# Last feed-forward of a four-layer block: gate and up from moments of the token rows, down weights in the order of the groups

## The reference, cut to what matters

```python
def spline_reconstruct(control_points, out_size, in_size):
    idx, f = _catmull_rom_grid(control_points.shape[0], out_size * in_size)
    ...  # w: cubic in f from four neighbouring control points
    return w.reshape(out_size, in_size)
gate = jnp.einsum('bsh,ih->bsi', hidden_states, gate_w)
up = jnp.einsum('bsh,ih->bsi', hidden_states, up_w)
inter = jax.nn.silu(gate) * up
return jnp.einsum('bsi,hi->bsh', inter, down_w)
```

## Time and profile before

| | |
|---|---|
| three runs | 2403.79, 2404.9, 2405.71 us |
| profiled execution, its span | 2401.79 us, 2400.0 us |
| mean granted TensorE clock | 0.981 of 2.4 GHz |
| TensorE, its weight loads | 2245.5 us (94%), 1246.9 us (52%) |
| VectorE, ScalarE, POOL | 1133.1 (47%), 866.2 (36%), 175.4 us (7%) |
| chain that ended last | PE 81%, DVE 11%, ACT 4%, issue 2%, DMA 1% |
| last feed-forward | 2085 to 2400 us |

### The profile page before, as it was taken

The page is one execution under the profiler, slowest core; times in us unless marked ns, Lnnn a source line. Parts: engine busy times, 40 slices in busy tenths (PEclk is TensorE's granted clock), DMA queues, the critical chain, the costliest instruction groups (busy, mean ns, idle before and its releaser), DMA issues.

```text
span 2400.0 us, 25795 instructions
## 1 busy us (share of the span) xinstructions
PE 2245.5 (94%) x9444; PEld 1246.9 (52%) x9444; DVE 1133.1 (47%) x2367; ACT 866.2 (36%) x1697; POOL 175.4 (7%) x356
## 2 busy tenths in 40 slices
PE   8999999999998989999999999968877888799999
PEld 3555554556664445555555556634434555444444
DVE  1433434474223855556555557755445666411111
ACT  1323332312221644545454445533333555311111
POOL 0000100000000211111101001000000000000000
PEclk9999999998999999999999999989988999999999
DMA  5444443334523311100000122010020111000000
GB/s 221 169 142 183 174 170 139 155 126 138 185 79 110 130 42 58 59 24 23 20 26 20 32 78 96 14 35 19 10 85 13 52 52 59 12 1 9 5 9 9
DMA packets 52513, 178.88 MB, mean 75 GB/s; under 512 B 5457, under 2 KB 25233, under 8 KB 46590
## 3 DMA queue, kind: packets, MB, share of 16 engines
q1 hardware_dynamic: 50662, 139.49, 16.9%
q0 software_dynamic: 1728, 37.75, 4.1%
HBM read 121.58 MB, written 46.47 MB: 70 GB/s over the span
## 4 chain that ended last, share of the span: by engine, by line
PE 81%; DVE 11%; ACT 4%; issue 2%; DMA 1%; SPq 0%; POOL 0%; DVEq 0%; ACTq 0%; POOLq 0%
PE psum L119 64%; PE psum L112 7%; PE psum L1468 5%; PE psum L1513 4%; DVE small L2300 2%; ACT WK L2258 1%; PE psum L1056 1%; DVE R L1223 1%; PE psum L2227 1%; DVE R L1222 1%; DVE R L1794 1%; DMA R<-in_wkv 1%; DVE WK L251 0%; DVE small L228 0%; DVE WK L1213 0%
## 5 line engine op out<-in xcount | busy, mean ns | idle before, releaser
L119 PE MATMUL psum<-R,WK 128*125 128x512 f32 (+7 forms) x3536 | 1325.2, 523 | 28.4 <-DMA WK<-in_ctxT 7.4
L119 PEld LDWEIGHTS psum<-R,WK 128*112 128x112 f32 (+4 forms) x3536 | 594.6, 174 | 687.3 <-issue 566.8
L112 PE MATMUL psum<-small,WK 112*125 112x112 f32 (+5 forms) x2036 | 280.7, 267 | 90.3 <-ACT WK L2264 28.5
L112 PEld LDWEIGHTS psum<-small,WK 112*125 112x125 f32 (+5 forms) x2036 | 228.7, 154 | 192.9 <-issue 92.5
L119 PE MATMUL psum<-WK,R 128*112 128x375 f32 (+3 forms) x704 | 221.0, 453 | 10.5 <-DVE R L1794 7.0
L1644 DVE TENSOR_REDUCE small<-psum 112x1 f32<-112x487 f32 x128 | 85.0, 664 | 194.4 <-PE psum L119 191.2
L119 PE MATMUL psum<-R 128*128 128x112 f32 (+3 forms) x960 | 158.7, 309 | 17.4 <-DVE R L1794 16.2
L119 PEld LDWEIGHTS psum<-WK,R 128*112 128x112 f32 (+2 forms) x704 | 111.8, 171 | 84.7 <-issue 14.8
L119 PEld LDWEIGHTS psum<-R 128*128 128x128 f32 (+3 forms) x960 | 116.1, 184 | 56.2 <-issue 26.2
L1468 PE MATMUL psum<-R,WK 128*112 128x512 f32 x256 | 120.1, 592 | 0.0
L1563 ACT ACTIVATE WK<-psum,small 112x487 f32<-112x487 f32 x128 | 97.0, 758 | 54.1 <-DVE small L1646 53.1
(11 more groups left out here) (214 smaller groups left out, 2126.7 us busy)
## 6 DMA issues: line engine op xcount, KB each, us to landing
R<-in_wf POOLq DMA_DIRECT2D x6, 4096.0 KB, 14.1
d_w<-R POOLq DMA_DIRECT2D x6, 2048.0 KB, 18.6
R<-d_w SPq DMA_DIRECT2D x6, 2048.0 KB, 11.2
WK<-in_ctxT SPq DMA_DIRECT2D x16, 750.0 KB, 5.6
d_v<-WK SPq DMA_DIRECT2D x16, 750.0 KB
R<-in_wq SPq DMA_DIRECT2D x7, 1024.0 KB, 7.3
R<-in_wo SPq DMA_DIRECT2D x6, 1024.0 KB, 17.1
d_k<-X SPq DMA_DIRECT2D x8, 750.0 KB, 3.2
```

The lines of the kernel that those rows point to most:

```text
L112: ins = pe.transpose(dst, src, idn[0:k, 0:k])
L119: ins = pe.matmul(dst, lhs, rhs, start=k == 0, stop=k == len(pairs) - 1)
```

## The change

The 2048 rows of gate and up are sorted by where their knots lie and cut greedily into groups of at most 128 rows, whose knots in each of the four 128-column pieces fall on at most seven positions (`spline_windows`). For a group, 32 functions of the column per piece (1, q, q squared, q cubed, and the same four cut off at each of seven positions) span all rows. In the last stage TensorE first multiplies the transposed token block by these functions (`feature`: four products of 32 output partitions per group, one per piece), which gives 128 moments per token (`fT`); gate and up of the group are then one product over these 128 moments with the group's coefficient rows (`gate_up`). The dense gate and up weights are no longer built; their 80 units are gone, and 48 are left, five per iteration of stage 4. The coefficient rows are stored once (`d_feat`), fetched in the order of the groups (`load_rows`, in stage 3, ahead of `back`), spread over the positions by VectorE (`which`, `row_of`, in iterations 3 to 7 of stage 4, behind the residual add; `moments`, the functions themselves, in iteration 8), and transposed in stage 5 (`turn_rows`, `keep_columns`). POOL writes the positions (`places`). As h now comes in the order of the groups, the down weights, built as before, are stored to DRAM behind stage 4 (`store_down`) and fetched in that order in stage 6, a seventh behind the V load of each sequence from the second on (`turn_down`). In the last stage the down products are cut in four parts with the moments of the next block between them, SiLU is one ScalarE activation straight from PSUM, and VectorE multiplies once.

```diff
+NPOS, NFEAT = 7, 32
...
+    found = []
+    members, held = [], [set()] * KT
+    for f in sorted(range(F), key=phase):
+        more = grown(held, f)
+        if len(members) == P or max(len(h) for h in more) > NPOS:
+            found.append((members, held))
+            members, more = [], grown([set()] * KT, f)
+        members.append(f)
+        held = more
+    found.append((members, held))
...
         d_ws = dram("d_ws", [2, T, D])
-        d_cgu = dram("d_cgu", [84, 16, 5 * P], BF16)
+        d_feat = dram("d_feat", [F, KT * 17])
+        d_wd = dram("d_wd", [F, D])
         d_cd = dram("d_cd", [84, 16, 3 * P], BF16)
...
-                    for dst, src in ((d_cgu, coefT[0:84, k % 8, 0:5]), (d_cd, coefT[0:84, k % 8, 5:8])):
-                        sp.dma_start(dst[:, k], src.rearrange("p s q -> p (s q)")).then_inc(sem(f"coef_stored{k % 8}"), 16)
+                    sp.dma_start(d_cd[:, k], coefT[0:84, k % 8].rearrange("p s q -> p (s q)")
+                                 ).then_inc(sem(f"coef_stored{k % 8}"), 16)
...
+                sp.wait_ge(sem("rows_ready"), 1)
+                sp.dma_start(d_feat.rearrange("(c p) e -> p c e", p=P), feat.rearrange("p (c k) e -> p c (k e)", k=KT)
+                             ).then_inc(sem("rows_stored"), 16)
                 for b in range(2, NB):
...
                     transposes(pe, [(dst[:, m * P:(m + 1) * P],
                                      split[:, m, 4 * k:4 * k + 4].rearrange("p t m i -> p (t m i)"))
-                                    for m in range(8)], identb).then_inc(act_ring.sem_filled, 1)
+                                    for m in range(3)], identb).then_inc(act_ring.sem_filled, 1)
...
+        FILLS = [range(2 * k, min(2 * k + 2, NV)) for k in range((NV + 1) // 2)]
+        turned_wd = Area(R0, 8192).get(WF, ft=FT, e=D)
+        features = Area(R0, 16384).get(NV * P, v=NV, k=KT, e=NFEAT)
+        columns = Area(R0, 19456).get(2 * F)
...
+            units = [(k, t) for k in range(16) for t in (None, 0, 1)]
...
+            def load_rows(sp):
+                for v, (_, _, _, blocks) in enumerate(windows):
+                    for at, f, width, high in blocks:
+                        src = bass.AP(tensor=d_feat.tensor, offset=f * 68, ap=[[243 * 68, high], [35 * 68, width], [1, 68]])
+                        sp.dma_start(taken[at:at + width * high, v].rearrange("p k e -> p (k e)"), src
+                                     ).then_inc(sem("spline_taken"), 16)
...
+            def store_down(sp):
+                sp.wait_ge(sem("spline_second"), pieces_upto[-1])
+                sp.dma_start(d_wd.rearrange("(c p) e -> p c e", p=P), wd).then_inc(sem("spline_wd_stored"), 16)
+            def turn_down(sp, part):
+                if part == 0:
+                    sp.wait_ge(sem("spline_wd_stored"), 16)
+                    sp.wait_ge(sem("spline_columns"), len(FILLS))
+                for v in range(NV):
+                    if v * 7 // NV != part:
+                        continue
+                    for at, high, width, f in row_pieces(v):
+                        src = bass.AP(tensor=d_wd.tensor, offset=f * D, ap=[[243 * D, high], [35 * D, width], [1, D]])
+                        sp.dma_start(turned_wd[at % P:at % P + high * width, at // P], src
+                                     ).then_inc(sem("spline_turned"), 16)
...
                 if u == 0:
-                    pe.wait_ge(sem("spline_cgu"), 16)
-                if (k, t) == (16, None):
                     pe.wait_ge(sem("spline_cd"), 16)
...
+            def which(dve, link):
+                dve.wait_ge(sem("spline_places"), 1)
+                dve.wait_ge(sem("spline_taken"), 16 * block_count)
+                for j in range(1, NPOS):
+                    ins = dve.tensor_scalar(place_of[:, 0:NV - 1, :, j], place_of[:, 0:NV - 1, :, j], float(j), None, ALU.add)
+                link(ins)
...
+            def prepare(dve, i):
+                link = dve_chain.on(dve)
+                if i == 3:
+                    which(dve, link)
+                if 4 <= i < 8:
+                    for e in range(4 * (i - 4), min(4 * (i - 3), 14)):
+                        ins = row_of(dve, e // NPOS, e % NPOS)
+                    if i == 7:
+                        ins.then_inc(sem("spline_rows"), 1)
+                        dve.wait_ge(sem("spline_rows"), 1)
+                if i == 8:
+                    moments(dve, link)
...
+            def turn_rows(pe, k):
+                if k >= len(FILLS):
+                    return
+                if k >= 2:
+                    pe.wait_ge(sem("spline_columns"), k - 1)
+                first = windows[FILLS[k][0]][0]
+                for v in FILLS[k]:
+                    at, count = 2 * (windows[v][0] - first), windows[v][1]
+                    ins = transposes(pe, [(place(k)[:, at + w * count:at + (w + 1) * count],
+                                           rows[0:count, v, w].rearrange("p k e -> p (k e)")) for w in range(2)], ident)
+                ins.then_inc(sem("spline_turned_rows"), 1)
+            def keep_columns(act, k):
+                if k >= len(FILLS):
+                    return
+                act.wait_ge(sem("spline_turned_rows"), k + 1)
+                first, last = windows[FILLS[k][0]], windows[FILLS[k][-1]]
+                n = 2 * (last[0] + last[1] - first[0])
+                act.copy(columns[:, 2 * first[0]:2 * first[0] + n], place(k)[:, 0:n]).then_inc(sem("spline_columns"), 1)
+            def whole(pe):
+                pe.wait_ge(sem("spline_columns"), len(FILLS))
+                pe.wait_ge(sem("spline_features"), 1)
...
-                        for u in range(3):
-                            spline["pe"](pe, 88 + 5 * i + u)
+                        spline["turn_rows"](pe, 2 * i)
...
+                    if b:
+                        spline["turn_down"](sp, b - 1)
...
+            act_ring, dve_ring = rings(stage, act_banks, act_order, dve_banks + [7], dve_order + [("y", 2)], tiles=NT)
...
+                def gate_up(b, k):
+                    if k == 0:
+                        for q in range(quads):
+                            (dve_ring if q % 2 else act_ring).wait_drained(pe, b, f"f{q}")
+                    dve_ring.wait_free(pe, b, f"u{k}")
+                    for v in FILLS[k]:
+                        at, count = windows[v][0], windows[v][1]
+                        to = 256 * (v % 2)
+                        ins = product(pe, dve_ring.bank[f"u{k}"][:, to:to + 2 * count],
+                                      [(fT[:, v, :], columns[:, 2 * at:2 * (at + count)])])
+                    ins.then_inc(dve_ring.sem_filled, 1)
+                def feature(b, q):
+                    ring = dve_ring if q % 2 else act_ring
+                    ring.wait_free(pe, b, f"f{q}")
+                    for v in range(4 * q, min(4 * q + 4, NV)):
+                        for kt in range(KT):
+                            ins = product(pe, ring.bank[f"f{q}"][kt * NFEAT:(kt + 1) * NFEAT, (v % 4) * P:(v % 4 + 1) * P],
+                                          [(features[:, v, kt, :], xnT[:, kt, :])])
+                    ins.then_inc(ring.sem_filled, 1)
...
                 for b0, b1, b2 in iterations(3, NT):
-                    if b1 == 0:
-                        x_ready(pe, n)
-                        pe.wait_ge(sem("spline_second"), spline["whole"])
-                    for c in range(FC):
+                    if b2 == 0:
+                        pe.wait_ge(sem("spline_turned"), 16 * spline["turned_count"])
+                    for c, part in enumerate((range(0), range(0, 3), range(3, 6), range(6, pairs))):
+                        if b2 is not None:
+                            turn_h(b2, c)
...
+                            for k in part:
+                                gate_up(b1, k)
...
+                        if b0 == 0:
+                            x_ready(pe, n)
+                            spline["whole"](pe)
+                    for q, part in enumerate((range(0, 6), range(6, 8), range(8, 10), range(10, FT))):
+                        if b2 is not None:
+                            down(b2, part)
+                        if b0 is not None and q < 3:
+                            if q == 0:
+                                act_ring.wait_drained(pe, b0, "xnT")
+                            for k in range(2 * q, 2 * q + 2):
+                                feature(b0, k)
...
+                def gate(b, k):
+                    dve_ring.wait_filled(act, b, f"u{k}")
+                    for v in FILLS[k]:
+                        count, to = windows[v][1], 256 * (v % 2)
+                        ins = act.activation(th[:, (pairs * b + k) % 3, P * (v % 2):P * (v % 2) + count],
+                                             dve_ring.bank[f"u{k}"][:, to:to + count], ACT.Silu)
+                    ins.then_inc(sem(f"{stage}_gate"), 1)
...
+                        for k, fill in enumerate(FILLS):
```

(16 more changed lines are left out.)

330 lines of the change are left out of this document (198 added, 132 removed).

## The result

| | us |
|---|---|
| before, 4 runs | 2404.35 (2403.79 to 2405.71) |
| after, 4 runs | 2271.18 (2268.84 to 2273.82) |
| ratio, 95% interval | 0.9446 (0.9429 to 0.9462) |
| profiled execution, its span | 2270.31, 2268.5 |

What follows compares the result with a forecast made beforehand. TensorE was taken to bound the last feed-forward. Last stage -94, linear attention +0.8, ternary layer -12.5 and first attention -4 gave -110 us: 2291.9 us from the profiled 2401.8, 2295 at the median; range 2274 to 2330.

Steps and rivals of the forecast that it cites:

- the wait for cd: Start of linear attention: TensorE's first product waits until table cd is loaded into a region freed late, +10.4 us.
- four clean streams: Last stage: moment records run in four array quarters at once without loss, 5.7 us per block; low end of the range.
- I take four with a little lost: 6.5 us per block: Last stage: moment products overlap across four array quarters, costing 6.5 us per block, 45.5 us in all.
- (a): Rival, last stage: only two moment streams run at a time, 11.4 instead of 6.5 us per block, +34, 2329 us; chance 0.14.
- (c): Rival, last stage: the moments do not overlap at all, 18.0 us per block, +80, 2375 us; chance 0.03.
- 5 us lost: Last stage's first two iterations: uncovered drains about 3 us, Silu's activation table 1.3, a half-clock stretch about 1.
- 1.1 us per iteration, seven are alike: Middle of linear attention: eight reconstruction units become five, saving 1.1 us per iteration, 7.7 us in all.
- my 3.9: End of linear attention: from the sixth sequence's add to the end 16.0 us instead of 19.9, a gain of 3.9.
- The +2 for iteration 3: Linear attention: VectorE's added `prepare` work, about 4.5 us with 3.6 covered by a product, costs +2 us.
- The 3 us that I took off for half-clock stretches: Ternary layer: the forecast gain was reduced by 3 us for stretches at half clock, leaving -12.5 us.
- First attention: First attention: coefficient transposes per group fall from eight to three in 16 groups, 80 x 0.05 = -4 us.
- 0.96 us each at most: Second ternary feed-forward: SP's 125 row-fetch DMAs cost at most 0.96 us each, 120 of 170 us, covered.

Runs made afterwards that it cites:

- the unaltered kernel: The kernel after the change, run once more without edits beside other runs on one chip: 2266.39 us (ratio 0.9433).
- the one-quarter run: Kernel after, with the moment products of each bank ordered quarter by quarter (all groups of quarter 0, then 1, 2, 3): 2308.56 us (0.9606).

## Why the prediction was wrong

The mechanism was right, no rival took place, and the largest terms came out: gate and up (7.0 us a block against 6.9), the wait for cd (+11.8 against +10.4), the untouched last attention. The forecast was 22 us short between the profiled executions, by sizes that nearly all missed on one side. The low end of the range, 2274, was called that of four clean streams, but by my own 5.7 us a block these give only 5.6 us less than 2295, so the rest of that end was not accounted for.

1. *Moments.* The step "I take four with a little lost: 6.5 us per block" failed: 5.0 us, -10.5 us in seven. The reason was a misread row. From the earlier trace rows I concluded that two quarters run beside each other, 0.059 us a record, and that one alone would cost 0.107. The record starts in that row come in pairs 95 to 120 ns apart: the two records of one product start together, the two quarters take turns, and 0.19 us before the next full-width matmul are part of the 0.71 us. One quarter alone costs 0.060 to 0.066 us. So the row does not show two quarters at work at once and does not bear out tiles in parallel, as I wrote it did; that four quarters overlap came true by luck and not by this row. (a) and (c) were overpriced as well: by my prices two quarters come to 6.4 us a block more than the 5.0 measured, +45 us, and one to 13.0 more, +91; the runs have +11 and +42 (both against the 2266.39 us of the unaltered kernel). Two quarters cost 6.5 us a block, the number that I had set for four. The Trainium skill, "TensorEngine Tiling (Array Packing)", section Theoretical Speedup, had the better price with its "up to 4x" for 32 columns: 3.6 by the runs. The Trainium skill's section Key Properties there speaks of different tiles working in parallel; the one-quarter run shows that this is only a part of the gain.
2. *Start-up.* "5 us lost" in the last stage failed. A block gains 43.9 - 28.47 = 15.43 us, and from the stage's length less seven blocks the start lost nothing: -109.6 + 7 x 15.43 = -1.6 us. Its parts were there: TensorE waits 2.5 us in the whole stage, and its first 168 moment records, partly at half clock, take 2.3 us longer than the next 168 (7.3 against 5.0). The activation table for Silu took 1.28 us of ScalarE, but TensorE did not wait for it. The stage of the kernel before had its own waits (4.6 us by ScalarE's and VectorE's hand-overs, 4.3 of them in the earlier trace rows) and a clock of 0.95 in its first 39.6 us, and I set nothing of that against mine. -6.6 us.
3. *Linear attention.* "1.1 us per iteration, seven are alike" failed twice. In the five steady iterations the gain was 0.9 us in all (81.4 to 80.5). The part of the removed units that stood between the output product and the next q product had filled a hand-over that is there without them: before, 0.43 us of waiting for the add (the row below); now 0.66. From the start of the output product to that of the q product 4.5 and 4.6 us pass. But iterations 0 to 3 gained 7.4 us, and the end 7.7 us against my 3.9, since there few products cover a unit (that reason is argued, not tested); the clock in the last stretch was 1.00 instead of 0.83 as well. +11.8 - 7.4 - 0.9 - 7.7 = -4.2 us, where I had +0.8: -5.0 us. Units moved into these waits shorten a steady iteration by 1 us, which shows that the waits and not the units set it. The +2 for iteration 3 was a slip, since 4.5 us less 3.6 covered are 0.9; the iteration behind that add is 16.7 us long, 16.6 before. TensorE in the kernel before, from the output product on:

```profile
1693.56 3.61 PE L119 MATMUL psum<-R,WK 128*112 128x512 f32 x8
1697.01 0.60 PE L119 MATMUL psum<-R 84*128 84x128 bf16 x5
1698.05 3.66 PE L119 MATMUL psum<-R,WK 128*112 128x512 f32 x8 [0.43 <-DVE X L260]
```

4. *Ternary layer.* The period was right to 0.2 us. The 3 us that I took off for half-clock stretches did not occur: the clock was 1.00 in the layer, 0.92 before. -3.6 us.
5. *First attention.* -6.2 us against -4. In the other profiles of kernels after this point lies at 759.2 to 762.4, so the miss is less than their spread. Not tested.
6. *Second ternary feed-forward.* Forecast 0, measured +3.7 us, by longer stretches at half clock that come and go between kernels with the same stage.
7. *Queues and POOL.* "0.96 us each at most" was cautious, 0.49 us by the row; hidden as forecast. POOL's 108 fills took under 4 us where I had 21.

Points 1 to 4 give -10.5, -6.6, -5.0 and -3.6 us, 5 and 6 -2.2 and +3.7. With +0.8 from the two stages between, and 1.2 us by which the rest of seven blocks came out longer than I had it (blocks -9.3, moments -10.5), that is the 22 us. In the rest of a block the 0.5 us of waits are gone, and the changes of width took their place, 0.6 us that I had put at nothing.

## What to carry to other kernels

Before a group of a few narrow matmuls is used as a price, look at the starts of its single records: a mean over 12 records hides which ones overlap and how much is the change to the next form. Where an engine already waits, removed filler gives nothing; count the removed instructions where the pipeline fills and empties, and expect little from its steady part. A table that a stage needs in its first instruction is worth a free corner of memory one stage earlier: 11 us here, a twelfth of the whole change.

## What the runs showed of the hardware

- A float32 matmul of 128 rows, 32 output partitions and 128 columns costs 0.060 to 0.066 us a record in one quarter of the array, 0.030 with four quarters in turn; at full width it is 0.112. A change between full width and narrow records costs time of its own: 0.19 us on the four down records before each narrow group, and 0.20 us from the start of the last narrow record to the next full-width one.
- With four quarters in turn the time goes with the token columns: four records start every 0.109 us at 128 columns, every 0.056 at 64. The issue of the eight instructions of a step (four weight loads, four matmuls) was not the limit.
- After one and the same wait of 3.4 us the same code went on at full clock (1.00 from 1435 to 1440 us), or at the lower level for a shorter or a longer while (0.93, 0.50), from execution to execution; the stage differs by up to 3.7 us (170.0 to 173.8). The last attention differs by up to 3 us in the same way (clock 0.95 and 0.93).
